# Cross-attention with four key groups: the value products of two key tiles in one burst, twice a unit, and the other steps placed around the bursts

## The reference, cut to what matters

```python
q = heads(x @ to_q_w)
h = [sdpa(q, heads(c_g @ to_k_g), heads(c_g @ to_v_g)) for each of the four groups g]   # softmax(q k / sqrt(32)) v
out = (h[0] + h[1] + h[2] + h[3]) @ to_out_w + to_out_b + x
```

## Time and profile before

| what | us |
|---|---|
| median of 3 runs (2624.28 to 2626.66) | 2626.12 |
| the profiled execution's own time | 2634.56 |
| its span, first to last instruction | 2632.5 |
| TensorE busy | 2526.2 (96%) |
| ScalarE busy | 1716.9 (65%) |
| VectorE busy | 1621.9 (62%) |
| GpSimd busy | 408.0 (15%) |

### The profile page before, as it was taken

The page is one execution under the profiler, slowest core; times in us unless marked ns, Lnnn a source line. Parts: engine busy times, 40 slices in busy tenths (PEclk is TensorE's granted clock), DMA queues, the critical chain, the costliest instruction groups (busy, mean ns, idle before and its releaser), DMA issues.

```text
span 2632.5 us, 37371 instructions
## 1 busy us (share of the span) xinstructions
PE 2526.2 (96%) x13125; PEld 1843.3 (70%) x13125; DVE 1621.9 (62%) x2964; ACT 1716.9 (65%) x3830; POOL 408.0 (15%) x564
## 2 busy tenths in 40 slices
PE   8999999999999947999999999999999999999997
PEld 8999999999999933455655556556555555556554
DVE  3131111111111138899898898898998998899881
ACT  3131222121211127999999999999999999999992
POOL 0000000000000012122122132132132221222210
PEclk9999999999999968999999999999999999999998
DMA  9473333232323246566666667566576666666641
GB/s 231 126 237 128 116 113 125 102 127 101 126 98 125 77 108 133 107 137 139 130 140 140 126 142 143 121 147 142 115 153 140 118 149 142 120 144 146 121 100 54
DMA packets 287618, 341.25 MB, mean 130 GB/s; under 512 B 89406, under 2 KB 181694, under 8 KB 287430
## 3 DMA queue, kind: packets, MB, share of 16 engines
q1 hardware_dynamic: 234032, 275.93, 46.7%
q10 hardware_dynamic: 53398, 62.93, 7.4%
HBM read 186.71 MB, written 83.89 MB: 103 GB/s over the span
## 4 chain that ended last, share of the span: by engine, by line
PE 54%; ACT 4%; DVE 4%; issue 2%; DMA 1%; SPq 0%; DVEq 0%
PE st_ps L808 11%; PE m_ps L843 11%; PE s_ps L794 11%; PE m_ps L866 11%; PE o_ps L822 10%; ACT probs L913 2%; ACT s_ps L921 2%; DVE negmax L977 1%; DVE neglse L1010 1%; DVE neglse L1005 0%; DVE neglse L1008 0%; DVE small L984 0%; DMA small<-in_group_rows 0%; DMA qpack<-q_out 0%; DVE kpack L963 0%
## 5 line engine op out<-in xcount | busy, mean ns | idle before, releaser
L921 ACT ACTIVATE s_ps<-s_ps,negmax 128x427 f32<-128x427 f32 x1280 | 764.5, 604 | 74.1 <-DVE small L984 74.0
L977 DVE TENSOR_REDUCE negmax<-s_ps 128x2 f32<-128x854 f32 x640 | 665.3, 1039 | 126.7 <-PE s_ps L794 124.9
L913 ACT ACTIVATE probs<-st_ps 128x1024 f32<-128x1024 f32 x640 | 662.2, 1035 | 74.4 <-PE st_ps L808 66.4
L794 PE MATMUL s_ps<-kpack,qpack 96*128 96x512 f32 x1280 | 426.2, 415 | 39.1 <-ACT s_ps L921 32.8
L464 PE MATMUL v_ps<-w_split,ctx_split 128*128 128x320 f32 (+2 forms) x3072 | 453.7, 309 | 1.4 <-DVE w_split L386 1.4
L464 PEld LDWEIGHTS v_ps<-w_split,ctx_split 128*128 128x128 f32 (+2 forms) x3072 | 451.4, 186 | 2.4 <-DVE w_split L386 1.7
L447 PE MATMUL k_ps<-ctx_split,w_split 128*128 128x428 f32 (+2 forms) x2280 | 428.0, 349 | 4.5 <-DVE ctx_split L386 4.5
L808 PE MATMUL st_ps<-qpack,kpack 104*128 104x512 f32 x1280 | 419.1, 409 | 13.7 <-ACT probs L913 12.0
L447 PEld LDWEIGHTS k_ps<-ctx_split,w_split 128*128 128x128 f32 x2280 | 410.2, 189 | 19.8 <-DVE ctx_split L386 4.8
L794 PEld LDWEIGHTS s_ps<-kpack,qpack 96*128 96x128 f32 x1280 | 230.1, 191 | 227.1 <-issue 115.6
L391 DVE TENSOR_TENSOR k_out<-k_ps,k_out 128x427 fp32r<-128x427 f32 (+2 forms) x97 | 56.1, 578 | 530.8 <-ACT k_out L287 530.8
(11 more groups left out here) (54 smaller groups left out, 1460.5 us busy)
## 6 DMA issues: line engine op xcount, KB each, us to landing
kpack<-kT SPq DMA_DIRECT2D x240, 256.0 KB, 5.4
qpack<-q_out SPq DMA_DIRECT2D x240, 256.0 KB, 5.7
kT<-k_out ACTq DMA_DIRECT2D x160, 217.5 KB, 2.2
ctx_split_raw<-in_ctxT SPq DMA_DIRECT2D x128, 214.0 KB, 4.4
xs_raw<-in_xT SPq DMA_DIRECT2D x80, 256.0 KB, 5.8
out<-in_xT SPq DMA_DIRECT2D x80, 256.0 KB, 6.2
out_yT<-out SPq DMA_DIRECT2D x80, 256.0 KB, 3.4
v_ip_rows<-v_out ACTq DMA_DIRECT2D x48, 320.0 KB
```

Of the source, the lines that this page charges most:

```text
L794: last = nc.tensor.matmul(s_ps[:, n % 2, z, :], qpack[0:ROWS_S, r, j, t * P:(t + 1) * P], kpack[0:ROWS_S, r, j, :], start=True, stop=True)
L913: nc.scalar.activation(probs[:, at:at + 2, :], st_ps[:, :, :], ACT.Exp).then_inc(p_done, 1)
L921: last = nc.scalar.activation(s_ps[:, n % 2, z, SMALL:TOK], s_ps[:, n % 2, z, SMALL:TOK], ACT.Exp, bias=negmax[:, r, IP, j, t:t + 1], accu ...
L977: nc.vector.tensor_reduce(negmax[:, r, IP, j, t0:t0 + 2], s_ps[:, n % 2, :, SMALL:TOK], AX_X, ALU.max, negate=True).then_inc(s_max, 1)
```

## The change

- `values` of key tiles 0 and 1 run back to back in step 2, those of 2 and 3 in step 6. They ran one by one in steps 0, 2, 4 and 6. The ring of probabilities grows from 6 to 10 tiles. To make room VR goes from 3 to 2, OR from 2 to 1, and `neglse` is written into `logs`.
- `queries` take five matmuls in each of steps 3, 4 and 5. `output` takes five in step 7 of slot w + 9 and five each in steps 0 and 1 of slot w + 10. Before, `queries` had 7, 2 and 6 in steps 5 to 7, and `output` 6, 2 and 7 in steps 1 to 3 of slot w + 9.
- DVE: both parts of heads move to step 0 a slot later, `keep_queries` from step 0 of the next slot to step 6 of its own, `add_output` from step 4 to step 2 of the next slot, ahead of `neg_lse`; the second `small_max` from step 6 to 7.
- ACT: `small_exp` moves from steps 4 and 7 to steps 4 and 0, `logs_of` to the front of step 2. POOL: `less_max` likewise to steps 4 and 0, ahead of that step's `split_x`; the fifth `split_x` goes from step 5 to step 4.
- SP: the order of a slot is now `load_values`, `pack_lse`, `store_output`, `load_x` (all five chunks, in the slot before the batch), `pack_keys`, `pack_queries`, `load_residual`. With one output buffer the residual's load waits for the store of the output before (`y_out`).
- The last five residuals go to x_raw, all at once, and their outputs are stored from there. There is one slot more at the end. The wait of `heads_hi` for room in heads is on `y_first`, set after the first three matmuls of an output, where it would wait for `y_done`.

```diff
--- before.py
+++ after.py
-VR = 3
-OR = 2
+VR = 2
+SR = 2
+OR = 1
 HR = 9
-PR = 6
+PR = 10
...
-Q_STEPS = {5: (0, 7), 6: (7, 9), 7: (9, 15)}
-X_STEPS = {0: (0,), 1: (1,), 2: (2,), 3: (3,), 5: (4,)}
-X_EARLY = 3
+PV_STEPS = {2: (0, 1), 6: (2, 3)}
+Q_STEPS = {3: (0, 5), 4: (5, 10), 5: (10, 15)}
+X_STEPS = {0: (0,), 1: (1,), 2: (2,), 3: (3,), 4: (4,)}
 Y_LAG = 9
-Y_STEPS = {1: (0, 6), 2: (6, 8), 3: (8, 15)}
+Y_FIRST = {7: (0, 5)}
+Y_REST = {0: (5, 10), 1: (10, 15)}
...
+LAST = UNITS - QC
...
+            def load_last_residuals():
+
+                sp.wait_ge(q_acc, UNITS)
+                for c in range(QC):
+                    sp.dma_start(x_raw[:, c, :], d["xT"][BATCH - 1, c * P:(c + 1) * P, :]).then_inc(res_last[c], 16)
...
             def slot(m):
-                if unit(m - Y_LAG):
-                    load_residual(m - Y_LAG)
-                if m > 0 and m % QC == 0 and unit(m):
-                    load_x(m, range(X_EARLY, QC))
-                if unit(m - 1):
-                    pack_queries(m - 1)
                 if unit(m - 3):
+                    load_values(m - 3)
                     pack_lse(m - 3)
...
-                if unit(m - 2):
-                    load_values(m - 2)
-                if unit(m - Y_LAG):
-                    store_output(m - Y_LAG)
+                if unit(m - Y_LAG - 1):
+                    store_output(m - Y_LAG - 1)
+                if (m + 1) % QC == 0 and unit(m + 1):
+                    load_x(m + 1, range(QC))
                 if m > 0 and unit(m):
                     pack_keys(m)
-                if (m + 1) % QC == 0 and unit(m + 1):
-                    load_x(m + 1, range(X_EARLY))
+                if unit(m):
+                    pack_queries(m)
+                if 0 <= m - Y_LAG < LAST:
+                    load_residual(m - Y_LAG)
+                if m == UNITS:
+                    load_last_residuals()
...
@@ gpsimd @@
                 for k in range(STEPS):
+                    if k == 0 and unit(m - 3):
+                        less_max(m - 3, 1)
+                    if k == 4 and unit(m - 2):
+                        less_max(m - 2, 0)
                     if m % QC == 0 and unit(m):
                         for c in X_STEPS.get(k, ()):
                             split_x(m, c)
-                    if k in (4, 7) and unit(m - 2):
-                        less_max(m - 2, k // 7)
...
@@ tensor @@
-                    if k % 2 == 0 and unit(m - 4):
-                        values(m - 4, k // 2)
+                    if unit(m - 4):
+                        for kt in PV_STEPS.get(k, ()):
+                            values(m - 4, kt)
                     products_at(m, k)
...
@@ scalar @@
                 for k in range(STEPS):
+                    if k == 2 and unit(m - 3):
+                        logs_of(m - 3)
                     u, duo = duo_at(m, k)
                     if unit(u):
                         prob(u, duo)
-                    if k == 2 and unit(m - 3):
-                        logs_of(m - 3)
                     u, p = pair_at(m, k)
                     if unit(u):
                         ip_sums(u, p)
-                    if k in (4, 7) and unit(m - 2):
-                        small_exp(m - 2, k // 7)
+                    if k == 0 and unit(m - 3):
+                        small_exp(m - 3, 1)
+                    if k == 4 and unit(m - 2):
+                        small_exp(m - 2, 0)
...
@@ vector @@
                 for k in range(STEPS):
-                    if k == 7 and unit(m - 4):
-                        heads_hi(m - 4)
                     u, p = pair_at(m, k)
                     if unit(u):
                         pair_max(u, p)
-                    if k == 0 and unit(m - 1):
-                        keep_queries(m - 1)
+                    if k == 0 and unit(m - 5):
+                        heads_hi(m - 5)
+                        heads_lo(m - 5)
                     if k == 1 and unit(m - 3):
                         small_sums(m - 3, 1)
+                    if k == 2 and unit(m - Y_LAG - 1):
+                        add_output(m - Y_LAG - 1)
                     if k == 2 and unit(m - 3):
                         neg_lse(m - 3)
                         turn_lse(m - 3)
-                    if k in (3, 6) and unit(m - 2):
-                        small_max(m - 2, k // 6)
-                    if k == 4 and unit(m - Y_LAG):
-                        add_output(m - Y_LAG)
+                    if k in (3, 7) and unit(m - 2):
+                        small_max(m - 2, k // 7)
                     if k == 5 and unit(m - 2):
                         small_sums(m - 2, 0)
-                    if k == 7 and unit(m - 4):
-                        heads_lo(m - 4)
+                    if k == 6 and unit(m):
+                        keep_queries(m)
...
@@ vector, heads_hi and add_output @@
-                    dve.wait_ge(y_done, (u - HR) // QC * QC + QC)
+                    dve.wait_ge(y_first if u % QC == HR % QC else y_done, (u - HR) // QC * QC + QC)
...
-                dve.wait_ge(res_in[w % OR], 16 * use(w, OR))
-                nc.vector.scalar_tensor_tensor(out=out[:, w % OR, :], in0=m_ps[:, :],
-                                               scalar=bias[:, w % QC:w % QC + 1], in1=out[:, w % OR, :],
+                if w < LAST:
+                    dve.wait_ge(res_in[w % OR], 16 * use(w, OR))
+                    to = out[:, w % OR, :]
+                else:
+                    dve.wait_ge(res_last[w % QC], 16)
+                    to = x_raw[:, w % QC, :]
+                nc.vector.scalar_tensor_tensor(out=to, in0=m_ps[:, :], scalar=bias[:, w % QC:w % QC + 1], in1=to,
```

More of the change, by code:

```diff
@@ L609, in attend @@
         o_hi, o_lo = sem("o_hi"), sem("o_lo")
-        y_done = sem("y_done")
+        y_first, y_done = sem("y_first"), sem("y_done")
         y_added = sem("y_added")
@@ L613, in attend @@
         y_out = [sem(f"y_out{r}") for r in range(OR)]
+        res_last, y_last = [sem(f"res_last{c}") for c in range(QC)], sem("y_last")
         def unit(u):
@@ L634, in small_stats @@
         def small_stats(tile, u, h):
-            s = tile[:, u % VR, :, PARTS[h][0]:PARTS[h][1], :].rearrange("p g j t -> p (j t) g")
+            s = tile[:, u % SR, :, PARTS[h][0]:PARTS[h][1], :].rearrange("p g j t -> p (j t) g")
             return s[:, :, 0], s[:, :, 1:IP]
@@ L711, in store_output @@
                 sp.wait_ge(y_added, w + 1)
-                sp.dma_start(d["yT"][b, rows, :], out[:, w % OR, :]).then_inc(y_out[w % OR], 16)
+                if w < LAST:
+                    sp.dma_start(d["yT"][b, rows, :], out[:, w % OR, :]).then_inc(y_out[w % OR], 16)
+                else:
+                    sp.dma_start(d["yT"][b, rows, :], x_raw[:, w % QC, :]).then_inc(y_last, 16)
             for c in range(QC):
@@ L771, in slot @@
                             split_x(m, c)
-                    if k in (4, 7) and unit(m - 2):
-                        less_max(m - 2, k // 7)
-            for m in range(UNITS + Y_LAG):
+            for m in range(UNITS + Y_LAG + 1):
                 slot(m)
@@ L827, in queries @@
                 if products[0] == 0:
-                    if unit(u - Y_LAG):
-                        pe.wait_ge(y_added, u - Y_LAG + 1)
+                    if unit(u - Y_LAG - 1):
+                        pe.wait_ge(y_added, u - Y_LAG)
                     elif u > 0:
@@ L856, in output @@
                     pe.wait_ge(o_lo, w // QC * QC + QC)
-                    if unit(w + Y_LAG - 1):
-                        pe.wait_ge(q_lo, w + Y_LAG)
+                    if unit(w + Y_LAG):
+                        pe.wait_ge(q_lo, w + Y_LAG + 1)
                     elif w > 0:
@@ L867, in output @@
                                             start=(n == 0), stop=(n == PRODUCTS - 1))
+                    if n == len(PASSES) - 1:
+                        last.then_inc(y_first, 1)
                 if products[-1] == PRODUCTS - 1:
@@ L874, in products_at @@
                     queries(m, range(*Q_STEPS[k]))
-                if k in Y_STEPS and unit(m - Y_LAG):
-                    output(m - Y_LAG, range(*Y_STEPS[k]))
+                if k in Y_REST and unit(m - Y_LAG - 1):
+                    output(m - Y_LAG - 1, range(*Y_REST[k]))
+                if k in Y_FIRST and unit(m - Y_LAG):
+                    output(m - Y_LAG, range(*Y_FIRST[k]))
             def slot(m):
@@ L937, in logs_of @@
                     act.wait_ge(lse_step, 3 * u)
-                nc.scalar.activation(logs[:, :, :, :], sums[:, u % VR, :, :, :], ACT.Ln).then_inc(ln_done, 1)
+                nc.scalar.activation(logs[:, :, :, :], sums[:, u % SR, :, :, :], ACT.Ln).then_inc(ln_done, 1)
             def slot(m):
```

23 lines of the change are left out of this document (12 added, 11 removed).

## The result

The kernel after takes 2690.31 us, the median of its runs (2685.54 to 2692.13), against 2626.32 for the kernel before beside it: a ratio of 1.0243, with the interval [1.0225, 1.026]. The profiled execution took 2688.88 in place of 2634.56, so the traces have 54.3 us to account for.

The account below looks back on a forecast made before the run. PE bounds the kernel, with ACT close behind. 64 plain units x -0.2 = -13, 15 batch units x 1.3 = +20, ends +2: +9 on 2634.56 gives 2643, less 8.4 for the profiled execution, 2635 us; range 2575 to 2690.

Parts of the forecast that it names:

- rival (c): Residual's load lands 9.6 us after q_out, late for DVE in every unit: +62 us, 2688; chance 0.22.
- Parts 1 and 2: PE: a doubled burst costs 2.12 us, two single ones 2.44; 0.64 saved a unit, which takes 18.50 without waits.
- Part 3: ACT lags behind PE after small_exp: 0.78 us of waiting, so a plain unit gains 0.2, not 0.64.
- The walk: Following ACT's lag behind PE step by step through a new plain unit: 18.50 + 0.78 + 0.18 = 19.46 us.
- rival (a): ACT catches up, the merging's gain comes through and PE runs at 18.6 us a unit: 2572; chance 0.24.
- Part 4: DVE's add_output waits for the residual queued behind the queries: no loss taken, at the other end 0.7 us a unit.
- Part 5: Unit that begins a batch: neg_lse meets POOL's splits, fifth split late, residual perhaps later; 22.3 us against 21.0 before.
- Rival (b): A batch's unit costs no more than before, plain units gain 0.2 to 0.4 us: 2602 to 2615; chance 0.16.
- Part 6: The ends: one more unit's output against shorter residual waits, +2 us; head of attend 0, plus or minus 3.

Follow-up runs that it names:

- e5: e2 with small_exp moved from short steps 0 and 4 to long steps 2 and 6, DVE's and POOL's steps following: 2582.86 us, ratio 0.9825.
- e8: e5 with its two doubled bursts taken apart into four single ones, in steps 2, 3, 6 and 7: 2614.90 us, ratio 0.9955.
- e1: The kernel after with the residual's load ahead of the queries' DMAs on SP: 2660.73 us, ratio 1.0121.
- e2: e1 with POOL's fifth split of x ahead of the less_max of step 4: 2644.28 us, ratio 1.0063.
- e4: e1 with hardly any work in small_exp (8 of 85 columns, logarithm replaced by a copy; work left out): 2624.70 us, ratio 0.9987.
- e9: e2 with POOL's subtraction in each split of x replaced by a copy (queries wrong): 2623.05 us, ratio 0.9980.
- e6: e2 with five unread matmuls in steps 7, 0 and 1 of slots 3 to 9, the fill: 2632.76 us, ratio 1.0014.

## Why the prediction was wrong

The forecast was 2635, and 2690.31 came, just beyond the end of the range. It came out near **rival (c)**, which gave 2688.

**Parts 1 and 2 (the bursts) held.** A doubled burst lasts 1.92, the range given. From the duo ahead of it to the duo behind it, less four matmuls, it costs 2.06 to 2.16 (e5, and the kernel after), against 2.12. Merging saves 0.36 each time (e8), the upper end of 0.30 to 0.36.

**Part 3 (ACT's lag) held.** The walk gave 19.46 for a plain unit, and 19.4 was taken; the shortest are 19.49 (e1, e2). The two waits in front of the long steps are there (0.37 and 0.20 in the rows above). With the longer duos behind them they cost 0.76 together (e4; 0.78 forecast). So rival (a) did not happen, for the reason given. What the walk had also said, and the text did not use, is that the 0.78 depends only on which steps hold `small_exp`. e5 moves it, and PE runs at 18.70.

**Part 4 is the step that failed.** Its numbers were right for the good units: the residual due 8.7 after q_out (8.8 measured), landing at 8.9 to 9.6 (8.9 in the good ones), with 0.2 free (0.2 measured). The step that failed is the one from these numbers to "I take 8.9 and no loss". It took the low end of the landing for every landing, and one due time for every unit. Where nothing is spare, the units that fall outside decide. In 19 plain units the load landed at 9.0 to 10.4; in nine more it landed at 8.9 and was due at 8.3. Half of the plain units so met a wait of 0.97, which is 0.43 a plain unit on average (19.95 here, 19.51 in e1, the first unit counted in both). The trace of before held a warning: the third of the query transfers in the earlier trace rows landed 7.6 after its issue in one unit and 6.9 in the other, a spread of 0.7 where 0.2 was free.

**Part 5 named the right waits, and left out one thing.** The forecast was 22.3, and the mean is 22.93. Taken apart by the runs: the plain unit 19.49; 1.97 more in e2, of which shorter POOL instructions take back 1.50 (e9; 1.6 to 1.8 forecast for POOL against `neg_lse`); 1.0 from e1 to e2; the residual 0.5 (e1), where "up to 2" was given and the two were rightly not added. The 1.0 fits the 0.9 taken for the fifth split only by luck: at full clock the split costs 0.37, and the other 0.6 is the granted clock, which fell in five of e1's fourteen batch units. The forecast had no term for the clock. The residual waited 2.48 on average in these units. Its removal gave only 0.5, which fits Part 5's argument that without it `neg_lse` waits for POOL instead. Rival (b) did not happen.

**Part 6 gave the start of attend "0, plus or minus 3"; it cost 10.** I looked only at waits. With the output's matmuls moved from steps 1 to 3 into the short steps 7, 0 and 1, these steps are empty until the first output exists; PE stands still in them, and the granted clock falls to 0.86 over 108 us. In the kernel before it was 0.98 with about as much idle time (10.0 of 98.6, against 12.9 of 108.5). e6 shows the cause by filling the gaps. The end came 4 better than the +2 forecast (-1.9), and no run asks why.

**The sum.** By cause, in the profiled executions: the residual's place 31 (e1), what is left of the batch units 14 x 1.48 = 21, the fill 10, the end -2, the plain units without the residual 56 x (-0.09) = -5. That is 55, for 54.3. Rival (c) was 64 x 0.5 + 15 x 2 = 62; in the same terms it is 56 x 0.35 + 14 x 1.95 = 47, then the fill and the end. Its mechanism is right, for 30 us of it (e1), though the residual is late in half of the units and not in every one. That its number fits within 2 is luck. It had 15 too much in the units; the fill and the end, which it did not have, gave 8 of them back, and the other 7 were hidden by the 8.4 that it took off for the profiled execution, an excess that the kernel after did not have. Of the 0.72 a unit that merging the bursts brings once nothing else binds (e8), only 0.1 (19.60 to 19.49) reached the period of the kernel after, even in the units that nothing disturbed.

## What to carry to other kernels

A load moved behind others on a queue must be judged by the spread of its landings, and of the times at which it is due, against the slack of the one who waits: with 0.2 us free, half of the units were late although the usual landing was in time. When bursts are merged, the steps become unequal, and every engine that runs beside them has to get its extra work in the long steps; here this decided over 60 us (2644 to 2583). And a change of the order of PE's work must be looked at in the fill too, where steps that look harmless may be empty. Time in which PE stands still can cost twice, once as waiting and once by the granted clock: look at the clock of each long unit before its length is put down to a wait.

## What the runs showed of the hardware

- Matmuls whose results nobody reads made the kernel 11.5 us faster, as they kept the granted clock at the full level (0.85 to 1.00 over 100 us). How much idle time there is does not decide alone: 10% of a stretch in the kernel before went with 0.98, 12% in the kernel after with 0.86.
- The granted clock fell in 6 of 14 batch units of the kernel after and in 5 of 14 of e1, where PE's waits were the same in all 14 (2.28 us of idle time). In e2, with 1.93 of idle time in such a unit, it was 1.00 in all 14.
- A DVE instruction of 64 columns took 0.27 alone and 1.39 beside a POOL subtraction of 512 columns (e2), and a copy of 512 columns on POOL was enough to make one of 0.22 last 0.52 (e9). The Trainium skill, "SBUF — State Buffer", section Who interferes with whom, says that the two engines share a port pair that is locked by one at a time; the first pair of numbers agrees with it.
- One going back and forth less between the layouts of 128 x 128 and of four 128 x 32 tiles was worth about 0.36 us (e5 to e8): 0.72 of a unit of 19.42.
- A 256 KB load behind three others on its queue landed 8.7 to 9.0 us after q_out in 36 plain units of the kernel after, and 9.0 to 10.4 in the other 19. In all of these a packet of an instruction queue began 1.0 to 8.2 us after q_out; that it is the cause is not shown.
